# Perceiver block: the group scales of the ternary feed-forward weights come from VectorE over a second load by rows, instead of a TensorE product with a block of ones

## The reference, cut to what matters

```python
w = w_fp32.astype(bfloat16)
w_g = w.reshape(-1, 64)                                  # 64 neighbours along the input dimension
scale = clip(mean(abs(w_g), axis=-1, keepdims=True), 1e-08, None)
q = clip(round(w_g / scale), -1, 1)
w_hat = (q * scale).reshape(w.shape)
return w + stop_gradient(w_hat - w)
```

## Time and profile before

| | |
|---|---|
| median of 3 runs | 1493.97 us (1493.25 to 1494.66) |
| profiled execution, its own time | 1493.47 us |
| span of its trace | 1491.5 us, 22107 instructions |
| DMA traffic over the span | 105.21 MB, mean 71 GB/s |
| pieces quantised in the main loop | 48, from 107.3 us to 1060.7 us |

### The profile page before, as it was taken

The page is one execution under the profiler, slowest core; times in us unless marked ns, Lnnn a source line. Parts: engine busy times, 40 slices in busy tenths (PEclk is TensorE's granted clock), DMA queues, the critical chain, the costliest instruction groups (busy, mean ns, idle before and its releaser), DMA issues.

```text
span 1491.5 us, 22107 instructions
## 1 busy us (share of the span) xinstructions
PE 1471.7 (99%) x6913; PEld 1194.8 (80%) x6949; DVE 1238.7 (83%) x1942; ACT 986.7 (66%) x3719; POOL 165.5 (11%) x120
## 2 busy tenths in 40 slices
PE   8999999999999999999999999999999999999998
PEld 7777778888888888888888888888888877788787
DVE  8758888989888988899889988998898899777643
ACT  5676776776776767667766766776677666556432
POOL 3210000002000200020011002000200210123342
PEclk9999999999999999999999999999999999999999
DMA  6542221211121121112111111121011133841000
GB/s 202 162 138 71 78 64 53 67 36 57 60 61 43 55 61 56 46 54 65 55 40 62 57 55 45 56 62 48 25 56 43 34 107 105 266 185 59 1 1 29
DMA packets 86660, 105.21 MB, mean 71 GB/s; under 512 B 7304, under 2 KB 67728, under 8 KB 85392
## 3 DMA queue, kind: packets, MB, share of 16 engines
q1 hardware_dynamic: 79248, 96.46, 20.9%
q10 hardware_dynamic: 7296, 7.34, 1.5%
HBM read 81.24 MB, written 22.54 MB: 70 GB/s over the span
## 4 chain that ended last, share of the span: by engine, by line
PE 85%; DVE 9%; issue 2%; ACT 2%; DMA 0%; POOL 0%; SPq 0%; ACTq 0%; DVEq 0%; POOLq 0%
PE ps L36 27%; PE ps L37 25%; PE ps L38 25%; DVE ring L1172 3%; PE ps L934 2%; PE ps L935 2%; DVE p_lo L42 2%; PE ps L952 1%; PE ps L953 1%; ACT ps L1741 1%; PE ps L807 1%; DVE ring L1143 0%; ACT recip L1778 0%; DMA wq_raw<-in_wq 0%; PE ps L564 0%
## 5 line engine op out<-in xcount | busy, mean ns | idle before, releaser
L1741 ACT ACTIVATE ps<-ps 123x128 f32<-123x128 f32 (+1 forms) x1248 | 326.2, 261 | 141.6 <-PE ps L38 141.4
L36 PE MATMUL ps<-wk_hi,cT_hi 128*128 128x512 f32 x832 | 329.0, 395 | 1.6 <-ACT sq L1735 1.4
L37 PE MATMUL ps<-wk_lo,cT_hi 128*128 128x512 f32 x832 | 325.9, 392 | 0.0
L38 PE MATMUL ps<-wk_hi,cT_lo 128*128 128x512 f32 x832 | 323.9, 389 | 0.0
L1741 ACT ACTIVATION_READ_ACCUMULATOR ps<-ps 123x1 f32 (+1 forms) x1248 | 232.0, 186 | 0.0
L36 PEld LDWEIGHTS ps<-wk_hi,cT_hi 128*128 128x128 f32 x832 | 156.3, 188 | 38.9 <-issue 3.6
L38 PEld LDWEIGHTS ps<-wk_hi,cT_lo 128*128 128x128 f32 x832 | 156.3, 188 | 34.1
L37 PEld LDWEIGHTS ps<-wk_lo,cT_hi 128*128 128x128 f32 x832 | 156.6, 188 | 32.3
L36 PE MATMUL ps<-p_hi,cn_hi 123*128 123x512 f32 (+1 forms) x400 | 164.7, 412 | 0.0
L36 PE MATMUL ps<-fq_hi,cT_hi 128*128 128x512 f32 x416 | 162.2, 390 | 0.6 <-DVE w_scale L1260 0.4
L38 PE MATMUL ps<-fq_hi,cT_lo 128*128 128x512 f32 x416 | 161.9, 389 | 0.0
(11 more groups left out here) (241 smaller groups left out, 2702.9 us busy)
## 6 DMA issues: line engine op xcount, KB each, us to landing
cT_raw<-in_ctxT SPq DMA_DIRECT2D x96, 128.0 KB, 3.6
cn_raw<-in_ctx SPq DMA_DIRECT2D x88, 123.0 KB
w_raw<-in_wguT SPq DMA_DIRECT2D x32, 256.0 KB, 2.7
qk_scratch<-folded ACTq DMA_DIRECT2D x8, 896.0 KB, 4.2
fq_raw<-qk_scratch SPq DMA_DIRECT2D x14, 512.0 KB, 3.8
pc_scratch<-pc_out SPq DMA_DIRECT2D x7, 1024.0 KB, 4.2
ternary_scratch<-w_out SPq DMA_DIRECT2D x48, 128.0 KB, 1.7
w_raw<-in_wpT SPq DMA_DIRECT2D x16, 256.0 KB, 2.6
```

The costliest lines, as they stand in the source:

```text
L36: pe.matmul(dst, l_hi, r_hi, start=first, stop=False)
L37: pe.matmul(dst, l_hi, r_lo, start=False, stop=False)
L38: return pe.matmul(dst, l_lo, r_hi, start=False, stop=last)
L1741: done = act.activation(head, head, ACT.Square, accum_out=k_sum[0:n, i, g * GH + h:g * GH + h + 1])
```

## The change

A second copy of the weights is handed in untransposed (`wgu`, `wp`) and loaded as 48 row pieces of 128 x 512, output rows on the partitions, so that a group lies along the free dimension. ACT takes the absolute values (`rows_abs`), DVE reduces eight groups of 64 per partition (`row_groups`: a `tensor_reduce` and a `tensor_scalar` of 128 x 8, and for every fourth row piece a `transpose` of 128 x 128 bfloat16). SP stores the turned scales to DRAM, four DMAs per block of four pieces (32 runs of 64 bytes each), and loads them back for each piece with two DMAs, each of which copies one row of 512 scales onto 64 partitions. The five instructions of `ternary_round` stay and read `w_scale[:, i % 3]`. The product on PE, its bank and both of its waits on PE go, and with them `group_ones`.

Row pieces 0 to 5 are done in steps 1 to 6; from step 7 on, a step with piece i also has row piece i + 6 (while there is one). The pieces now start at step 7 and take seven steps of a batch, t = 3, 5, 6, 8, 9, 11 and 12, the last one in step 89. So five batches have three pairs of adjacent steps with a piece each, where before they had one pair.

The row buffers lie over `resid`, so x is loaded a second time after the last piece. The three bias loads share one semaphore. The numbers of the `consts` waits shift. The core of the diff:

```diff
+        scale_dram = nc.dram_tensor("scale_scratch", [3 * NJ, BANK // GROUP, BANK], BF16, kind="Internal").ap()
...
-        group_ones = lasting.take("group_ones", [P, P], BF16)
...
-        w_scale = work.take("w_scale", [P, BANK], BF16)
+        row_abs = work.take("row_abs", [P, BANK], BF16)
+        over = Region(nc, resid_at, resid_at + 8 * KIB)
+        row_raw = over.take("row_raw", [P, BANK])
+        w_scale = over.take("w_scale", [P, 3, BANK], BF16)
+        row_sum = over.take("row_sum", [P, BANK // GROUP])
+        row_scales = over.take("row_scales", [P, 4, 32], BF16)
+        row_turned = over.take("row_turned", [P, 4, 32], BF16)
...
+        row_pieces = []
+        for j in range(NJ):
+            for first in (j * BANK, FF + j * BANK):
+                row_pieces += [wgu[first + i * P:first + (i + 1) * P, :] for i in range(4)]
+            row_pieces += [wp[i * P:(i + 1) * P, j * BANK:(j + 1) * BANK] for i in range(4)]
...
-        piece_slots = list(range(2, TT + 1)) + [b * TT + t for b in range(1, B - 1) for t in (3, 5, 6, 8, 10, 12)]
+        ROW_LEAD = 6
+        piece_slots = list(range(ROW_LEAD + 1, TT + 1)) + [
+            b * TT + t for b in range(1, B - 1) for t in (3, 5, 6, 8, 9, 11, 12)][:NP - TT + ROW_LEAD]
...
+        row_at = {s: s - 1 for s in range(1, ROW_LEAD + 1)}
+        row_at.update({s: i + ROW_LEAD for s, i in piece_at.items() if i + ROW_LEAD < NP})
+        spread_at = {ROW_LEAD - 1: 0, ROW_LEAD: 1}
+        spread_at.update({s: i + 2 for s, i in piece_at.items() if i + 2 < NP})
...
-            def ternary_groups(s, i):
-                pe.wait_ge(consts, 6)
-                pe.wait_ge(w_abs_sgn, 2 * i + 1)
-                pe.wait_ge(scaled, s)
-                pe.matmul(bank(S_BANK), group_ones[:], w_abs[:], start=True, stop=True).then_inc(w_groups, 1)
...
-                    if s in piece_at:
-                        pe.wait_ge(w_steps, 5 * piece_at[s] + 1)
...
-                    if g == 3 and s in piece_at:
-                        ternary_groups(s, piece_at[s])
...
-            def ternary_scale(i):
-                dve.wait_ge(w_groups, i + 1)
-                dve.tensor_scalar(w_scale[:], bank(S_BANK), 1.0 / GROUP, 1e-8, ALU.mult, ALU.max).then_inc(w_steps, 1)
+            def row_groups(r):
+                dve.wait_ge(row_abs_done, r + 1)
+                dve.wait_ge(row_steps, row_count(r, 0))
+                dve.tensor_reduce(row_sum[:], row_abs[:].rearrange("p (g e) -> p g e", e=GROUP), AX_X,
+                                  ALU.add).then_inc(row_steps, 1)
+                dve.wait_ge(row_steps, row_count(r, 1))
+                dve.tensor_scalar(row_scales[:, r % 4, 0:BANK // GROUP], row_sum[:], 1.0 / GROUP, 1e-8, ALU.mult,
+                                  ALU.max).then_inc(row_steps, 1)
+                if r % 4 == 3:
+                    dve.wait_ge(row_steps, row_count(r, 2))
+                    if r > 3:
+                        dve.wait_ge(row_stored, 4 * 16 * (r // 4))
+                    dve.transpose(row_turned[:].rearrange("p i n -> p (i n)"),
+                                  row_scales[:].rearrange("p i n -> p (i n)")).then_inc(row_steps, 1)
             def ternary_round(i):
-                first = 5 * i
-                dve.wait_ge(w_steps, first + 1)
+                first, scale = 4 * i, w_scale[:, i % 3]
+                dve.wait_ge(scale_in, 2 * 16 * (i + 1))
+                dve.wait_ge(w_abs_sgn, 2 * i + 1)
                 if i > 0:
                     dve.wait_ge(w_out_done, i)
-                dve.scalar_tensor_tensor(out=w_q[:], in0=w_scale[:], scalar=257.0 / 512.0, in1=w_abs[:],
+                dve.scalar_tensor_tensor(out=w_q[:], in0=scale, scalar=257.0 / 512.0, in1=w_abs[:],
                                          op0=ALU.mult, op1=ALU.is_lt).then_inc(w_steps, 1)
...
+                if s in row_at:
+                    row_groups(row_at[s])
...
+                dve.wait_ge(x_in[m], 2 * 16)
...
+            def rows_abs(r):
+                act.wait_ge(row_in, 16 * (r + 1))
+                if r > 0:
+                    act.wait_ge(row_steps, row_count(r - 1, 1))
+                act.activation(row_abs[:], row_raw[:], ACT.Abs).then_inc(row_abs_done, 1)
...
+                if s in row_at:
+                    rows_abs(row_at[s])
...
+            def load_rows(r):
+                if r > 0:
+                    sp.wait_ge(row_abs_done, r)
+                sp.dma_start(row_raw[:], row_pieces[r]).then_inc(row_in, 16)
+            def store_scales(blk):
+                sp.wait_ge(row_steps, row_count(4 * blk + 3, 3))
+                for a in range(4):
+                    sp.dma_start(scale_dram[blk].rearrange("g (i a n) -> a g i n", i=4, a=4)[a],
+                                 row_turned[32 * a:32 * a + BANK // GROUP]).then_inc(row_stored, 16)
+            def spread_scales(i):
+                sp.wait_ge(row_stored, 4 * 16 * (i // 4 + 1))
+                if i > 0:
+                    sp.wait_ge(scale_in, 2 * 16 * i)
+                if i >= 3:
+                    sp.wait_ge(w_out_done, i - 2)
+                for half in range(2):
+                    sp.dma_start(w_scale[half * GROUP:(half + 1) * GROUP, i % 3],
+                                 scale_dram[i // 4, 2 * (i % 4) + half].partition_broadcast(GROUP)).then_inc(scale_in, 16)
...
+            sp.wait_ge(ln_norm, MT)
+            load_rows(0)
...
+                if s == min(piece_at) - 1:
...
+                if s in row_at:
+                    r = row_at[s]
+                    if r + 1 < NP:
+                        load_rows(r + 1)
+                    if r % 4 == 3:
+                        store_scales(r // 4)
+                if s in spread_at:
+                    spread_scales(spread_at[s])
+                if s == max(piece_at) + 1:
+                    sp.wait_ge(row_stored, 4 * 16 * (NP // 4))
+                    for m in range(MT):
+                        sp.dma_start(resid[:, m, :], x_rows[m * P:(m + 1) * P, :]).then_inc(x_in[m], 16)
```

More of the change, by code:

```diff
@@ L89, in perceiver_block @@
         neg_half = lasting.take("neg_half", [P, 16])
+        resid_at = lasting.at
         resid = lasting.take("resid", [P, MT, DM])
@@ L299, in perceiver_block, with row_count @@
         NP = len(pieces)
+        row_pieces = []
[3 more added lines that the diff above has]
+            row_pieces += [wp[i * P:(i + 1) * P, j * BANK:(j + 1) * BANK] for i in range(4)]
         FQ_STEPS = (4, 7)
-        piece_slots = list(range(2, TT + 1)) + [b * TT + t for b in range(1, B - 1) for t in (3, 5, 6, 8, 10, 12)]
+        ROW_LEAD = 6
+        piece_slots = list(range(ROW_LEAD + 1, TT + 1)) + [
+            b * TT + t for b in range(1, B - 1) for t in (3, 5, 6, 8, 9, 11, 12)][:NP - TT + ROW_LEAD]
         piece_at = {s: i for i, s in enumerate(piece_slots)}
         assert len(piece_at) == NP and max(piece_at) < N
+        row_at = {s: s - 1 for s in range(1, ROW_LEAD + 1)}
+        row_at.update({s: i + ROW_LEAD for s, i in piece_at.items() if i + ROW_LEAD < NP})
+        spread_at = {ROW_LEAD - 1: 0, ROW_LEAD: 1}
+        spread_at.update({s: i + 2 for s, i in piece_at.items() if i + 2 < NP})
+        def row_count(r, step):
+            return 1 + 2 * r + r // 4 + step
         consts = sem("consts")
@@ L342, in perceiver_block @@
         part_steps = sem("part_steps")
-        w_in, w_abs_sgn, w_groups = sem("w_in"), sem("w_abs_sgn"), sem("w_groups")
+        w_in, w_abs_sgn = sem("w_in"), sem("w_abs_sgn")
+        row_in, row_abs_done, row_steps = sem("row_in"), sem("row_abs_done"), sem("row_steps")
+        row_stored, scale_in = sem("row_stored"), sem("scale_in")
         w_steps, w_out_done, w_stored = sem("w_steps"), sem("w_out_done"), sem("w_stored")
@@ L356, in perceiver_block @@
         wa_in = [sem(f"wa_in{i}") for i in range(4)]
-        bias_in = [sem(f"bias_in{i}") for i in range(3)]
+        bias_in = sem("bias_in")
         w_bf_in = sem("w_bf_in")
@@ L1154, in track_max @@
                     if b == 0:
-                        dve.wait_ge(consts, 8)
+                        dve.wait_ge(consts, 5)
                     else:
@@ L1201, in track_sum @@
                     if b == 0:
-                        dve.wait_ge(consts, 9)
+                        dve.wait_ge(consts, 6)
                     else:
@@ L1268, in ternary_round @@
                                          op0=ALU.mult, op1=ALU.is_lt).then_inc(w_steps, 1)
+                dve.wait_ge(w_steps, first + 1)
+                dve.tensor_tensor(w_q[:], w_q[:], scale, ALU.mult).then_inc(w_steps, 1)
                 dve.wait_ge(w_steps, first + 2)
-                dve.tensor_tensor(w_q[:], w_q[:], w_scale[:], ALU.mult).then_inc(w_steps, 1)
+                dve.tensor_tensor(w_q[:], w_q[:], w_abs[:], ALU.subtract).then_inc(w_steps, 1)
                 dve.wait_ge(w_steps, first + 3)
-                dve.tensor_tensor(w_q[:], w_q[:], w_abs[:], ALU.subtract).then_inc(w_steps, 1)
```

(29 more changed lines are left out.)

21 lines of the change are left out of this document (8 added, 13 removed).

## The result

The changed kernel takes 1483.36 us (median of 4 runs, 1483.00 to 1484.07), the kernel before 1493.61 (1492.95 to 1494.66): a ratio of 0.993 [0.9915, 0.9945], or 10.3 us faster. The forecast was 13.1 us less, 1480.9. The profiled execution took 1483.59 us with a span of 1481.4.

What follows compares the result with a forecast made beforehand. PE, busy for 99% of the span, was taken as the bound. 8.3 + 3.7 + 1.1 = 13.1 us off the profiled 1493.47 gave 1480.4, and 0.5 more for the median 1480.9; the range reached from 3 us below to 1486.

Steps and rivals of the forecast that it cites:

- 36 products at 0.23 us, 8.3: PE outside the fill: 36 pieces lose their group product of 0.23 us each, 8.3 us gained.
- doesn't do what it says: Rival, chance 0.04: the 0.23 us are a hand-over that stays; only 1.2 us of waiting go, 1492.8 us.
- Fill, 3.7: PE from step 2 to step 13: 11 group products (2.5 us) and 1.2 us of waiting go, 3.7 gained.
- Steps 13 and 14, counted as nothing: End of the fill: step 13's piece gains nothing, since its step ends in the chain of DVE's key_mean, which stays.
- 2.7 us of room: In the fill: DVE's scaled scores are ready at 194.3, PE asks at 197.0, so PE does not feel DVE's lag.
- The loop of the row loads, 7.4 us: Single row buffer, adjacent steps: ACT, DVE, store, landing of 2.8 us and hand-offs make 7.4 us, against 8.2 in the fill.
- signs of being wrong: A DVE reduce above 1.5 us, PE idle before key groups, or SP's row load issued over 3 us into the step.
- The ends of batches, 1.1: PE's idle at six batch ends falls from 0.60 to 0.41 us, 1.1 gained; bounds 3.6 gained or as much lost.
- DVE's terms: Reduce 0.72 us, scalar instruction 0.09, transpose 0.3; key_mean 1.5, at most 2.0, us behind PE's next step; no cost to PE.
- SP's terms: SP's queue: each issue about 0.37 us, at most 2.6 us more after a piece's store, costing nothing.
- the fill gives its part back: Rival, chance 0.18: DVE's lag or late row loads stop PE in steps 8 to 14; 4 us lost, 1484.9.
- The slower rival: Chance 0.04: row loads landing at 9.0 us hold up ACT in adjacent steps; 19 to 71 us slower, 1513 to 1565.

Runs made afterwards that it cites:

- e3: The kernel before without its group products and the waits on them, scales computed from a constant, no row pieces: 1479.72 us, ratio 0.9909 to before.
- e1: The changed kernel with SP issuing the next row load ahead of the piece load and the wait for w_out: 1482.14 us, ratio 0.9927 to before.
- e4: The changed kernel with DVE's tensor_reduce of each row piece done twice: 1488.40 us, ratio 0.9968 to before.
- e5: The changed kernel with the row load ahead of the wait for w_out and no piece in step 13: 1479.82 us, ratio 0.9909 to before.
- e2: The changed kernel without the piece and row piece of step 13, the 48th piece moved to step 90: 1481.64 us, ratio 0.9923 to before.

## Why the prediction was right and wrong

The sign, the mechanism on PE and the range (1477.9 to 1486.0) hold. The point is 2.5 us too low. Two terms are wrong in opposite directions, 2.8 us lost in steps 13 and 14 and 0.8 gained in the fill, so the point is nearer than its worst term deserves; the 0.6 us by which step 0 starts later is most of the rest. Term by term:

- **36 products at 0.23 us, 8.3: right.** Steps 16 to 90 are 9.1 us shorter; without the batch ends below that is 8.1 for the 36 products, 0.225 each. Pairs of adjacent steps take 10.99 each. The rival "doesn't do what it says" is out: e3 takes the product and the waits for it away, adds nothing, and gets the same steps.
- **Fill, 3.7: 0.8 too little.** Steps 2 to 12 gained 4.5. Before, they took 97.02; now 92.48 and no idle time, which is 0.227 per matmul of 408 where I had reckoned with 0.229. I took the length of a full step's matmul for one of the fill. A product cost more there than its 0.23, too: a step with one and without a wait took 8.43, now 8.16.
- **Steps 13 and 14, counted as nothing: the step that failed.** They cost 2.8. (The piece of step 13 alone was rightly counted as nothing, as e3 shows; the lag was not.) The prediction saw the lag ("so what `low_fq` adds in step 7, and the transposes in steps 8 and 12, stay as lag, some 1.5 us") and checked it against one consumer alone, PE's scores one step on, where 2.7 us of room were. That check holds for the fill: not a single stall before step 14 (in step 14 even the scores wait, 0.53 us). But the lag is also handed on to `key_mean` at the end of the fill, and that chain has no room: PE waited for ACT there before any change (0.48 us, the line of 211.32 above). There the delay is paid in full. The lag was also larger than 1.5: 2.8 at `key_mean` of step 13. The 1.5 itself was right for what it named, for with row loads in time (e1) the lag is 15.34 - 13.86 = 1.5; the other 1.35 came from the loads.
- **The loop of the row loads, 7.4 us: too short.** From the start of `row_abs` to the issue of the next row load are 4.4 to 4.7 us, and to its data another 3.4 to 4.2 in steps 8 to 12, where I had put 2.8 from the loads of the earlier trace rows. The turns took 8.14, 8.40, 8.64 and 8.61 us from step 8 to step 12, against PE's 8.16, so each late load is handed on. e1 prices this at 1.35 us. Two of the prediction's own signs of being wrong stood in the fill, and not in the pairs after it: ACT waited 1.1 to 1.9 us for `row_raw` in steps 8 to 12, and SP issued the row load 5.3 to 6.3 us into PE's step there.
- **The ends of batches, 1.1: right.** A gain of 1.1 was forecast from the nearest row, and 1.1 came: two steps at a batch's end take 22.19 to 22.29 instead of 22.41 to 22.43. In three of the six POOL's sum now meets `numerator_lo` first, as forecast, and either way DVE's subtraction ends at 7.61 to 7.66 us into the step, where it ended at 7.81.
- **DVE's terms.** The reduce takes 0.68 us recorded and 0.72 from start to start (forecast 0.72), the transpose 0.31 (0.3). `key_mean` stands 1.6 to 2.1 us behind PE's next step in pairs, 2.4 once (forecast 1.5 and at most 2.0). The rule of the Trainium skill, VectorE: DVE Perf Modes, section Rules for kernel authors, to expect 1x from `tensor_reduce`, agrees with the trace: 0.68 us from bfloat16 here, 0.68 from float32 in `key_mean`. Its advice to consider restructuring is for a reduce on the hot path, and outside the fill this one is not on it: e4 shows a second reduce to cost 1.4 us in 35 row pieces.
- **SP's terms.** Four stores of scales take 2.90 us to issue, 0.72 each, and two spreads 1.09, where I had 0.37 each. It costs PE nothing that a trace shows: between 95 and 1200 us the profile puts no engine's wait on a DMA other than a row load.
- **The rival "the fill gives its part back"**, priced at 4 us, is what happened, at 2.8 of it. I had given it 0.18 and should have given it more: it named the two loops, 8.2 and 7.4 against 8.2, and a loop that is as long as the step it hides behind cannot make up a lag again.
- **The slower rival**, row loads that land at 9 us, did not come: their median is 2.9 us, the longest of 48 took 6.6, and that one came before step 0. After step 13 ACT never waits for one. From the figure for an access under high load in the Trainium skill, DMA: Bandwidth & Descriptors, section Latency and other measured facts, the prediction had estimated a landing of 4.6 us. Two of the 48 loads took that long (4.64 and 6.58), the common one did not; those of the fill, at up to 4.2, come near it.

After the fix (e5) the gain is 1493.32 - 1479.82 = 13.5 us against 13.1. That is near for reasons that the sum did not have: it includes 1.2 us in steps 13 and 14 (16.32 instead of 17.52) from moving a piece, and the 0.8 more in the fill, and some of this is lost again before step 0 and after step 101.

What stays open: what made the one load of e2 late was not tried, nor an order that frees both DVE and POOL at the ends of batches, nor why `k_mean` of e5 and the small instructions of 128 x 8 take 1.2 to 1.5 us beside POOL's reduction.

## What to carry to other kernels

When work moves to an engine whose loop is already as long as the step that hides it, ask for every consumer of that engine until the stage ends, above all the last one: a lag that stops nobody for six steps is still paid where the next chain without room begins. A single buffer whose refill is issued behind another piece's store makes a loop of its own; add up its issue and its landing beside other transfers, and put the load ahead of the store if the sum comes near the step. And before moving an instruction out of a slow neighbour's way, look at what the move makes later and at what then takes its place beside the neighbour: here another instruction was held up instead, and the reduction itself became the one that PE's release hung on.
